# A selective scan whose delta·u·B product is formed on two engines

## The chip, the core and the metric

The program runs on one core of a Trainium2 chip. Time is the device time of one execution in microseconds (us). Before the change the median of three runs is 3355.29 us (3349.27 to 3361.40).

A core has a matrix engine (TensorE, PE in the profile; PEld is its weight load), VectorE (DVE), ScalarE (ACT), GpSimd (POOL) and SyncE (SP), each with an instruction stream of its own, which wait for one another on semaphores. TensorE writes to PSUM. VectorE and ScalarE read and write PSUM and SBUF; the GpSimd instructions of this kernel read and write SBUF alone.

## The reference, cut to what matters

The whole program is sixteen residual layers. The change is inside the first, a selective state-space scan (Mamba):

```
deltaA  = exp(delta * a)                # b l d n
deltaBu = delta * B * u                 # b l d n
step:  h = deltaA_t * h + deltaBu_t     # over the 256 positions of a sequence
       y = sum_n h * C_t
```

There are 8 sequences of 256 positions (2048 tokens), 256 inner channels d and 16 states n. B and C depend on token and state and are the same for every channel; delta and u depend on token and channel.

## The kernel before, in words

Channels lie on the 128 partitions, in M = 2 halves. Tokens are taken in 4 chunks c of C = 512 columns (two sequences each). For each chunk and each of the 16 states n there is one step q = 16 c + n, so there are Q = 64 steps. A step works on tiles of 128 partitions by 2 x 512 = 1024 columns:

- **TensorE** `spread` copies one row of B (then of C) to all 128 partitions with three bf16 matmuls of 512 columns, into the PSUM tiles `BB` and `CB` (L2431). There is one `BB` and one `CB`, so the next `spread` into `BB` waits until the product of the step before has read it. TensorE also sums the products with C over the 16 states into the PSUM tile `Y` (L2466, two float32 matmuls, four records), two steps late.
- **ScalarE** forms `dA[q]` = exp(delta · a) in two instructions (L2478), released when scan q-2 is done, and then copies `CB` to SBUF, `cb[q]` (L2484).
- **VectorE** forms `dBu[q]` = du · B with one `tensor_tensor` over all 1024 columns, which reads `du` from SBUF and `BB` from PSUM (`times_b`, L2518), and runs the recurrence with one `tensor_tensor_scan` (`scan`, L2527). It issues `times_b(q+1)` ahead of `scan(q)`.
- **GpSimd** forms `hc[q]` = hs · cb over 1024 columns in SBUF (L2493), after scan q.

`dBu`, `hs`, `cb`, `dA` and `hc` are double buffered. After the second step of each later chunk VectorE finishes the chunk before (`finish`: L2538, then L2543, whose two inputs `yv` and `gate` are both in SBUF). At steps 22, 38 and 54 TensorE projects that chunk into `BB` (`outputs`, L2440 and L2442) and VectorE adds it to x (`add_x`, L2548); there VectorE issues `scan(q)`, `add_x`, `times_b(q+1)` in that order. The last chunk is finished behind the loop. Nothing but the order in which each engine's block is written, and the semaphores, sets the order of the work.

## Time and profile before

| | |
|---|---|
| median of 3 runs | 3355.29 us |
| profiled execution, its own time | 3366.05 us |
| its span | 3364.3 us |
| mean granted TensorE clock | 0.894 |
| busy PE / DVE / ACT / POOL | 2804.9 / 2007.6 / 1387.5 / 962.4 us |

The span is from the first to the last instruction of the profiled execution. The scan stage that the change touches takes about 117 to 377 us of it; the other fifteen layers and the first half of this one take the rest and are not touched. In the rows below a line number is one of the kernel before; `x64` is a count; a time in square brackets behind a row of the timeline is how long the engine had been idle and who released it.

### The profile page before, as it was taken

The numbers are of one execution on the slowest core, as the hardware profiler recorded it, in microseconds if no ns is written. First come the engines' busy times: TensorE is split into PE (matmuls) and PEld (weight loads), VectorE is DVE, ScalarE is ACT, GpSimd is POOL, SyncE is SP. The second block draws the span as 40 slices with busy tenths as digits, with TensorE's granted clock in tenths as the row PEclk, the third lists the DMA queues.
The fourth block names the chain that finished last, engine by engine and source line by source line (L and its number), as shares of the span: only waits on it lengthen the run. The fifth ranks groups of instructions, "written<-read, shape, count | busy, mean of one in ns | idle before, by whom it ended". The sixth has DMA issues, their size and how long they took to land. (4 is left out here: it accounts for less than half of the span.)

```text
span 3364.3 us, 61234 instructions
## 1 busy us (share of the span) xinstructions
PE 2804.9 (83%) x23920; PEld 1857.1 (55%) x23920; DVE 2007.6 (60%) x4357; ACT 1387.5 (41%) x2886; POOL 962.4 (29%) x1321
## 2 busy tenths in 40 slices
PE   5589699979699969887687699996999969689996
PEld 2233367756477645555454566763566646456664
DVE  4999754556655566733465356665666646556664
ACT  4444244434244333322253244443555524345553
POOL 1355332223323220103213333331122235412222
PEclk7799799989799978777798799997999979799998
DMA  1000100000000000002010000001122101022221
GB/s 77 1 0 0 51 1 1 1 23 27 1 1 1 1 1 1 1 1 83 17 27 17 19 1 1 1 1 52 55 70 80 60 22 33 15 69 77 69 77 43
DMA packets 46939, 90.95 MB, mean 27 GB/s; under 512 B 6052, under 2 KB 34524, under 8 KB 45888
## 3 DMA queue, kind: packets, MB, share of 16 engines
q1 hardware_dynamic: 44608, 86.43, 8.4%
q8 instruction: 194, 3.18, 0.4%
q0 software_dynamic: 2048, 0.61, 0.1%
q14 instruction: 89, 0.73, 0.1%
HBM read 70.16 MB, written 19.14 MB: 27 GB/s over the span
## 5 line engine op out<-in xcount | busy, mean ns | idle before, releaser
L751 ACT ACTIVATE s_sT<-s_R 128x1024 f32<-128x1024 f32 (+2 forms) x448 | 400.1, 945 | 197.9 <-PE s_R L685 197.0
L786 DVE TENSOR_REDUCE s_negm<-s_R 128x4 f32<-128x1024 f32 x320 | 377.1, 1221 | 174.6 <-PE s_R L656 174.6
L656 PE MATMUL s_R<-s_qk 32*128 32x256 f32 (+2 forms) x3584 | 250.1, 394 | 62.7 <-ACT s_sT L751 33.5
L685 PE MATMUL s_R<-s_qA,s_qk 32*128 32x256 f32 (+2 forms) x3584 | 241.5, 383 | 16.1 <-DVE s_negm L786 10.7
L704 PE MATMUL s_OB<-s_sT,s_v 128*32 128x256 f32 (+2 forms) x3584 | 224.6, 368 | 10.0 <-ACT s_sT L751 6.4
L758 ACT ACTIVATE s_oc<-s_OB 128x256 f32<-128x256 f32 x224 | 86.0, 384 | 333.7 <-PE s_OB L704 333.7
L656 PEld LDWEIGHTS s_R<-s_qk 32*128 32x128 f32 x3584 | 158.7, 191 | 110.8 <-issue 88.5
L801 DVE TENSOR_TENSOR s_qA<-s_qk,s_X 128x256 f32<-128x256 f32 x224 | 94.3, 421 | 200.2 <-PE s_X L716 200.2
L2493 POOL TENSOR_TENSOR all_hT<-s0s_hs,s0s_cb 128x1024 f32<-128x1024 f32 x64 | 150.6, 2354 | 199.4 <-DVE s0s_hs L2527 182.2
L685 PEld LDWEIGHTS s_R<-s_qA,s_qk 32*128 32x128 f32 x3584 | 162.9, 185 | 78.4 <-issue 64.1
L1375 POOL TENSOR_TENSOR s_pr<-s_pr,s_rinv 128x1024 f32<-128x1024 f32 x64 | 121.3, 1895 | 224.7 <-DVE s_rinv L1481 224.7
L1453 ACT ACTIVATE s_pr<-s_S,s_negmax 128x256 f32<-128x256 f32 x256 | 118.7, 471 | 135.2 <-DVE s_negmax L1484 135.2
L791 DVE TENSOR_REDUCE s_negm<-s_R 128x2 f32<-128x256 f32 (+2 forms) x256 | 116.3, 518 | 68.2 <-PE s_R L666 68.1
L704 PEld LDWEIGHTS s_OB<-s_sT,s_v 128*32 128x32 f32 x3584 | 94.3, 109 | 106.7 <-issue 28.6
L2527 DVE TENSOR_TENSOR_SCAN s0s_hs<-s0s_dA,s0s_dBu 128x1024 f32<-128x1024 f32 x64 | 145.7, 2281 | 0.0
L2466 PE MATMUL s0s_Y<-all_hT,all_ident 128*128 128x512 f32 x256 | 129.7, 631 | 9.0 <-DVE s0s_yv L2538 6.3
L767 POOL TENSOR_SCALAR_AFFINE_SELECT s_sT<-s_sT 128x512 f32<-128x512 f32 x128 | 81.5, 637 | 176.7 <-ACT s_sT L751 174.7
L716 PE MATMUL s_X<-all_ident,s_negm 128*128 128x128 f32 x448 | 97.7, 300 | 14.5 <-DVE s_negm L786 7.6
L1064 POOL TENSOR_TENSOR s_veps<-s_mv,all_eps 128x2 f32<-128x2 f32 x64 | 16.7, 261 | 323.1 <-DVE s_mv L1266 323.1
L2431 PE MATMUL s0s_BB<-s0s_xparts,all_ident_bf 80*128 80x512 bf16 x192 | 57.9, 414 | 57.6 <-DVE s0s_xparts L2510 41.5
L1484 DVE TENSOR_REDUCE s_negmax<-s_S 128x4 f32<-128x1024 f32 x64 | 78.3, 1223 | 37.4 <-PE s_S L1393 37.4
L2484 ACT ACTIVATE s0s_cb<-s0s_CB 128x512 f32<-128x512 f32 x64 | 38.3, 598 | 138.3 <-PE s0s_CB L2431 137.1
(571 smaller groups left out, 6284.6 us busy)
## 6 DMA issues: line engine op xcount, KB each, us to landing
s_wB<-enc_b SPq DMA_DIRECT2D x32, 962.5 KB, 4.9
s_scratch<-s_pk SPq DMA_DIRECT2D x51, 256.0 KB, 2.0
s_qk<-s_scratch SPq DMA_DIRECT2D x204, 64.0 KB
s_wA<-enc_a SPq DMA_DIRECT2D x32, 193.0 KB, 4.1
big<-moe SPq DMA_DIRECT2D x2, 2347.0 KB, 11.2
big<-routed SPq DMA_DIRECT2D x2, 2084.0 KB
all_W<-weights SPq DMA_DIRECT2D x1, 2296.0 KB, 17.1
all_W<-weights SPq DMA_DIRECT2D x1, 2295.5 KB, 12.1
```

The source lines that it names most:

```text
L656: last = pe.matmul(S[h][:, t * T:t * T + hi - lo], b.qk[rows, r % 2, 0, c, t * P:(t + 1) * P], b.qk[rows, r % 2, 1, c, lo:hi], start=(t == ...
L685: last = pe.matmul(b.R[:, a.turned_at(u, h // 2), :][:, h % 2, a.at(kt)], b.qk[rows, r % 2, 1, c, kt * P:(kt + 1) * P], b.qA[rows, u % 2, ...
L704: last = pe.matmul(b.OB[32 * h:32 * (h + 1), lo:hi], b.v[:, r % 2, kt, a.HP * c + h, :], b.sT[:, j % (a.lag + 1), h, a.at(kt)], start=(kt ...
L716: last = pe.transpose(b.X[:, t * P:(t + 1) * P], b.negm[:, u % 2, t, :], g.ident[:])
L751: act.activation(b.sT[:, u % (a.lag + 1), 2 * p:2 * p + 2, 0:a.width], b.R[:, a.turned_at(u, p), 0:a.width], ACT.Exp).then_inc(s.expd, 1)
L786: ins = dve.tensor_reduce(b.negm[:, u % 2, :, at].rearrange("p t h -> p h t"), S.rearrange("p h (t k) -> p h t k", t=TT), AX_X, ALU.max, n ...
L791: ins = dve.tensor_reduce(b.negm[:, u % 2, t, at], S[:, :, t * T:t * T + hi - lo], AX_X, ALU.max, negate=True)
L1375: pool.tensor_tensor(p, p, rinv[:, u % 3, :, :].rearrange("p h t -> p (h t)").unsqueeze(2) .to_broadcast([P, 2 * TT, T]), ALU.mult).then_i ...
L1453: ins = act.activation(pr[:, u % 3, h, t, :], S[:, u % 2, h, t * T:(t + 1) * T], ACT.Exp, bias=negmax[:, u % 3, h, t:t + 1], accum_out=sum ...
L2466: last = pe.matmul(Y[:, m, :], g.ident[:], hc[:, j % 2, m, :], start=first, stop=last_)
L2493: pool.tensor_tensor(hc[:, q % 2, :, :], hs[:, q % 2, :, :], cb[:, q % 2, :].unsqueeze(1).to_broadcast([P, M, C]), ALU.mult)\
L2527: dve.tensor_tensor_scan(out=hs[:, q % 2, :, :].rearrange("p m c -> p (m c)"), data0=dA[:, q % 2, :, :].rearrange("p m c -> p (m c)"), dat ...
```

## The change

`bb` is a new SBUF tile of 128 x 2 x 144. ScalarE copies columns 368 to 511 of `BB` into it (`copy_b`), once per step, between its `exp` instructions and its copy of `CB`. GpSimd multiplies these 144 columns of both halves (288 of the 1024) by the copy (`times_b_high`), issued ahead of its `hc` product of the step before; VectorE's `times_b` keeps columns 0 to 367 (736 of 1024). The semaphore `dbu` becomes `dbu_low` and `dbu_high`, and `scan` waits for both. `times_b` now waits for ScalarE's copy (`bb_cp`), no longer for the matmuls, and TensorE waits for `dbu_low` alone before it overwrites `BB`.

```diff
--- before.py
+++ after.py
@@ -2401,6 +2401,8 @@
             dBu = ss.sb("dBu", [P, 2, M, C])
             hs = ss.sb("hs", [P, 2, M, C])
             cb = ss.sb("cb", [P, 2, C])
+            CUT = 368
+            bb = ss.sb("bb", [P, 2, C - CUT])
             xparts = ss.sb("xparts", [ROWS, 3, NTOK], BF16)
 
             hc = g.hT[:, 0:2 * M * C].rearrange("p (i m c) -> p i m c", i=2, m=M)
@@ -2410,9 +2412,9 @@
             BB = ss.ps("BB", [P, C])
             CB = ss.ps("CB", [P, C])
             Y = ss.ps("Y", [P, M, C])
-            split, cleared, bb_mm, cb_mm, cb_cp, exps, dbu, scans, hcs, summed, gated, out_mm, added = [
-                ss.sem(n) for n in ("split", "cleared", "bb_mm", "cb_mm", "cb_cp", "exps", "dbu", "scans", "hcs",
-                                    "summed", "gated", "out_mm", "added")]
+            (split, cleared, bb_mm, bb_cp, cb_mm, cb_cp, exps, dbu_low, dbu_high, scans, hcs, summed, gated, out_mm,
+             added) = [ss.sem(n) for n in ("split", "cleared", "bb_mm", "bb_cp", "cb_mm", "cb_cp", "exps", "dbu_low",
+                                           "dbu_high", "scans", "hcs", "summed", "gated", "out_mm", "added")]
             Q = NC_ * N
 
             def segments(t):
@@ -2447,7 +2449,7 @@
                     spread(BB[:], 0, 32, bb_mm)
                     for q in range(Q + 2):
                         if q + 1 < Q:
-                            pe.wait_ge(dbu, q + 1)
+                            pe.wait_ge(dbu_low, q + 1)
                             if (c := projects(q)) is not None:
                                 outputs(c)
                                 pe.wait_ge(added, c + 1)
@@ -2469,6 +2471,13 @@
 
                 @block.scalar
                 def _(act):
+                    def copy_b(q):
+                        act.wait_ge(bb_mm, q + 1)
+                        if q >= 2:
+                            act.wait_ge(dbu_high, q - 1)
+                        act.activation(bb[:, q % 2, :], BB[:, CUT:C], ACT.Copy).then_inc(bb_cp, 1)
+
+                    copy_b(0)
                     act.wait_ge(cleared, 1)
                     for q in range(Q):
                         c, n = divmod(q, N)
@@ -2478,6 +2487,8 @@
                             ins = act.activation(segments(dA[:, q % 2, m, :]), segments(delta[:, m, c * C:(c + 1) * C]),
                                                  ACT.Exp, scale=aneg[:, m * N + n:m * N + n + 1])
                         ins.then_inc(exps, 1)
+                        if q + 1 < Q:
+                            copy_b(q + 1)
                         act.wait_ge(cb_mm, q + 1)
                         if q >= 2:
                             act.wait_ge(hcs, q - 1)
@@ -2485,7 +2496,20 @@
 
                 @block.gpsimd
                 def _(pool):
+                    def times_b_high(q):
+
+                        c = q // N
+                        pool.wait_ge(bb_cp, q + 1)
+                        if q >= 2:
+                            pool.wait_ge(scans, q - 1)
+                        pool.tensor_tensor(dBu[:, q % 2, :, CUT:C], du[:, :, c * C + CUT:(c + 1) * C],
+                                           bb[:, q % 2, :].unsqueeze(1).to_broadcast([P, M, C - CUT]), ALU.mult)\
+                            .then_inc(dbu_high, 1)
+
+                    times_b_high(0)
                     for q in range(Q):
+                        if q + 1 < Q:
+                            times_b_high(q + 1)
                         pool.wait_ge(cb_cp, q + 1)
                         pool.wait_ge(scans, q + 1)
                         if q >= 2:
@@ -2512,16 +2536,18 @@
                     def times_b(q):
 
                         c = q // N
-                        dve.wait_ge(bb_mm, q + 1)
+                        dve.wait_ge(bb_cp, q + 1)
                         if q >= 2:
                             dve.wait_ge(scans, q - 1)
-                        dve.tensor_tensor(dBu[:, q % 2, :, :], du[:, :, c * C:(c + 1) * C],
-                                          BB[:].unsqueeze(1).to_broadcast([P, M, C]), ALU.mult).then_inc(dbu, 1)
+                        dve.tensor_tensor(dBu[:, q % 2, :, 0:CUT], du[:, :, c * C:c * C + CUT],
+                                          BB[:, 0:CUT].unsqueeze(1).to_broadcast([P, M, CUT]), ALU.mult)\
+                           .then_inc(dbu_low, 1)
 
                     def scan(q):
 
                         dve.wait_ge(exps, q + 1)
-                        dve.wait_ge(dbu, q + 1)
+                        dve.wait_ge(dbu_low, q + 1)
+                        dve.wait_ge(dbu_high, q + 1)
                         if q >= 2:
                             dve.wait_ge(hcs, q - 1)
                         dve.tensor_tensor_scan(out=hs[:, q % 2, :, :].rearrange("p m c -> p (m c)"),
```

## Rows read from the trace of the kernel before

**Rows 1.** Groups by line and shape, 100 to 380 us: busy, mean ns | idle before, releasers.

```profile
L2493 POOL TENSOR_TENSOR all_hT<-s0s_hs,s0s_cb 128x1024 f32<-128x1024 f32 x64 | 150.6, 2354 | 199.4 <-DVE s0s_hs L2527 182.2 <-PE s0s_Y L2466 16.0 <-ACT s0s_cb L2484 1.2
L2527 DVE TENSOR_TENSOR_SCAN s0s_hs<-s0s_dA,s0s_dBu 128x1024 f32<-128x1024 f32 x64 | 145.7, 2281 | 0.0
...
L2518 DVE TENSOR_TENSOR s0s_dBu<-s_du,s0s_BB 128x1024 f32<-128x1024 f32 x64 | 78.1, 1221 | 22.7 <-PE s0s_BB L2431 16.9 <-DVE s0s_hs L2527 0.5
...
L2484 ACT ACTIVATE s0s_cb<-s0s_CB 128x512 f32<-128x512 f32 x64 | 38.3, 598 | 138.3 <-PE s0s_CB L2431 137.1 <-POOL all_hT L2493 1.2
```

**Rows 2.** Timeline of one steady step, all engines: start us, us, engine, instruction.

```profile
226.13 1.30 ACT L2478 ACTIVATE s0s_dA<-s_delta,s_aneg 128x510 f32<-128x510 f32 x2
226.20 1.22 DVE L2518 TENSOR_TENSOR s0s_dBu<-s_du,s0s_BB 128x1024 f32<-128x1024 f32 x1
226.23 2.35 POOL L2493 TENSOR_TENSOR all_hT<-s0s_hs,s0s_cb 128x1024 f32<-128x1024 f32 x1 [1.17 <-DVE s0s_hs L2527]
227.33 2.28 DVE L2527 TENSOR_TENSOR_SCAN s0s_hs<-s0s_dA,s0s_dBu 128x1024 f32<-128x1024 f32 x1
...
227.47 0.82 PE L2431 MATMUL s0s_BB<-s0s_xparts,all_ident_bf 80*128 80x512 bf16 x3 [0.34 <-DVE s0s_dBu L2518]
...
228.13 0.81 PE L2431 MATMUL s0s_CB<-s0s_xparts,all_ident_bf 80*128 80x512 bf16 x3
...
228.78 1.88 PE L2466 MATMUL s0s_Y<-all_hT,all_ident 128*128 128x512 f32 x4
228.98 0.60 ACT L2484 ACTIVATE s0s_cb<-s0s_CB 128x512 f32<-128x512 f32 x1 [1.55 <-PE s0s_CB L2431]
...
229.72 1.22 DVE L2518 TENSOR_TENSOR s0s_dBu<-s_du,s0s_BB 128x1024 f32<-128x1024 f32 x1
```

**Rows 3.** Timeline of PE alone where it catches up.

```profile
274.19 0.81 PE L2431 MATMUL s0s_BB<-s0s_xparts,all_ident_bf 80*128 80x512 bf16 x3
...
277.21 0.81 PE L2431 MATMUL s0s_BB<-s0s_xparts,all_ident_bf 80*128 80x512 bf16 x3
```

**Rows 4.** Groups by shape, POOL, whole span.

```profile
L1088 POOL TENSOR_TENSOR s_x1b<-s_x,s_wB 128x256 f32<-128x256 f32 x32 | 21.3, 667 | 2.5
...
L2942 POOL TENSOR_TENSOR s1a_oh<-s1a_oh,s_sig 128x128 f32<-128x128 f32 x32 | 14.0, 438 | 0.0
...
L1370 POOL TENSOR_TENSOR all_x<-all_x,all_W 128x2048 f32<-128x2048 f32 x1 | 4.5, 4508 | 3.0 <-SPq L1367 3.0
```

**Rows 5.** Groups by shape, DVE and ACT, whole span.

```profile
L358 DVE TENSOR_TENSOR s_sT<-s_S,all_causal 128x512 f32<-128x512 f32 x32 | 21.7, 680 | 0.0
...
L2905 ACT ACTIVATE s1a_v<-s1a_F 128x256 f32<-128x256 f32 x32 | 12.3, 384 | 87.4 <-PE s1a_F L2807 87.4
```

**Rows 6.** Timeline at the finish of the first and of the last chunk.

```profile
184.58 2.35 POOL L2493 TENSOR_TENSOR all_hT<-s0s_hs,s0s_cb 128x1024 f32<-128x1024 f32 x1 [1.55 <-DVE s0s_hs L2527]
185.77 2.24 DVE L2543 TENSOR_TENSOR s0s_yv<-s0s_yv,s_gate 128x1024 f32<-128x1024 f32 x1
...
376.07 1.23 DVE L2543 TENSOR_TENSOR s0s_yv<-s0s_yv,s_gate 128x1024 f32<-128x1024 f32 x1
```

**Rows 7.** Timeline of DVE where it waited for `BB`.

```profile
131.30 1.22 DVE L2518 TENSOR_TENSOR s0s_dBu<-s_du,s0s_BB 128x1024 f32<-128x1024 f32 x1 [0.55 <-PE s0s_BB L2431]
...
212.09 1.22 DVE L2518 TENSOR_TENSOR s0s_dBu<-s_du,s0s_BB 128x1024 f32<-128x1024 f32 x1 [4.59 <-PE s0s_BB L2431]
...
275.05 1.22 DVE L2518 TENSOR_TENSOR s0s_dBu<-s_du,s0s_BB 128x1024 f32<-128x1024 f32 x1 [1.79 <-PE s0s_BB L2431]
```

**Rows 8.** Timeline of the last steps, DVE and POOL.

```profile
365.49 4.46 DVE L2527 TENSOR_TENSOR_SCAN s0s_hs<-s0s_dA,s0s_dBu 128x1024 f32<-128x1024 f32 x2
...
367.91 4.64 POOL L2493 TENSOR_TENSOR all_hT<-s0s_hs,s0s_cb 128x1024 f32<-128x1024 f32 x2 [1.18 <-DVE s0s_hs L2527]
```

**Rows 9.** Busy us by stretch: PE, PEld, DVE, ACT, POOL, granted clock, DMA share, GB/s.

```profile
117.00:370.00 253.00, 227.93 (x703) 93.54 (x701) 231.21 (x140) 117.32 (x190) 148.03 (x63) 0.92 0.00 0
...
184.00:192.00 8.00, 6.12 (x11) 2.42 (x12) 7.86 (x7) 1.85 (x4) 2.88 (x2) 0.57 0.00 0
```

## The prediction

> **What bounds the kernel now.** I read first the groups by line of the scan stage [rows 1], because the change touches nothing else: the 64 steps are in 117 to 370 us, 253 us of a span of 3364.3. In that stretch VectorE is busy 231.2 us and TensorE 227.9, at a mean granted clock of 0.92; GpSimd 148.0 and ScalarE 117.3 [rows 9]. Two engines near the full time don't say which one sets the pace, so I read the timeline of one step [rows 2]. VectorE's product starts at 226.20 and the next one at 229.72: 3.52 us per step. Between them it does 1.22 us of product and 2.28 us of scan, one right behind the other (the scan's record begins 0.09 before the product's ends; the next product begins 0.11 after the scan's end, 229.61). VectorE never waits: the scan group has 0.0 us of idle time before it over 64 instructions, and the product group 22.7 us, most of it at a few places [rows 1]. All others wait in each step: GpSimd 1.17 us for the scan, ScalarE 1.55 us for `CB`, TensorE 0.34 us for the product. So a steady step is VectorE's own work, and a shorter product shortens the step one for one until another engine becomes late. That next engine is to be found. TensorE, when it catches up without a wait at the full clock, needs 277.21 - 274.19 = 3.02 us per step [rows 3]. GpSimd needs 2.354 us, ScalarE 1.30 + 0.60 = 1.90.
>
> **What the change takes from VectorE.** Its product goes from 1024 to 736 columns. Two sizes with one PSUM and one SBUF operand are at hand: 1221 ns for 1024 [rows 1], 680 for 512 [rows 5]; that is 1.057 ns per column, and 1221 - 288 x 1.057 = 917 ns. I take 0.92 us, a gain of 0.30 us per step; the step of VectorE becomes 3.22 us. Bounds: if all of the time shrank with the columns the gain would be 0.34, and it can't be much under 288 x 1.0 ns = 0.29.
>
> **What it adds to GpSimd.** A product over 288 columns in SBUF. Sizes: 128 columns 438 ns, 256 columns 667, 2048 columns 4508 [rows 4]; from the last two, 2.14 ns per column and 118 ns fixed, so 118 + 617 = 735 ns. Lower bound 288 x 2.2 = 0.63 us (the longest piece's cost per column, nothing fixed), upper bound 288 x 3.42 = 0.99 us (the smallest piece's cost per column). I take 0.74, as 288 lies beside 256. Two GpSimd products run back to back without a gap, 4.64 us for two [rows 8], so GpSimd's step is 2.354 + 0.74 = 3.09 us, below VectorE's 3.22 with 0.13 to spare. At the upper bound it is 3.34, and GpSimd would be the bound.
>
> The Trainium skill's "GPSIMD Engine Reference", section "Engine selection", says to keep elementwise work on VectorE because two-input operations are about twice as slow on GpSimd. The rows above agree in the ratio (0.74 us for what VectorE does in 0.30, as one price against the other); by that rule the change loses 0.44 us of engine time per step, and by the row on GpSimd's 1.17 us of idle time that loss is covered.
>
> **What it adds to ScalarE.** A copy of 144 columns from PSUM: 256 columns take 384 ns [rows 5] and 512 take 598 [rows 1], 0.836 ns per column, so 290 ns. ScalarE's step is 1.90 + 0.29 = 2.19 us, far below 3.22. The question is the order. Count from E, the end of scan q-1, behind which `times_b(q+1)` should begin at E + 0.11. `times_b(q)` ended at about E - 2.2; the matmuls of `BB` follow at once and take 0.82 us [rows 2], so they end at E - 1.3, and the copy runs to E - 1.0. It stands behind exp(q) in ScalarE's queue; that was released by scan q-2 at E - 3.2 and is over at E - 1.9. The copy is thus 1.0 us early. Queued behind it is the copy of `CB` (its matmuls end at E - 0.7, so it starts when it did) and then the next exp, released at E. TensorE is free for `BB` in time: it waits for `hc`, which now ends 2.35 + 0.14 after a scan as before, and its 3.02 us fit in 3.22.
>
> **GpSimd's order.** Its stream is now `times_b_high(q+1)`, `hc(q)`. `hc(q-1)` starts at E + 0.14 and ends at E + 2.49, the new piece ends at E + 3.23, and `hc(q)` is released by scan q at E + 3.22 + 0.14. So it is just in time, 0.13 us early. Scan q+1, which needs the piece, starts some 0.9 us after its end: covered. If the piece costs p, the step is the larger of 3.22 and 2.354 + p.
>
> **A lock.** VectorE's L2543 has two SBUF inputs. It takes 1.23 us when GpSimd is idle and 2.24 us when it starts at 185.77 during a GpSimd product that ends at 186.93; 186.93 + 1.08 is its end [rows 6]. So it is held until the GpSimd product is over. VectorE's product in each step starts 0.03 us before a GpSimd product and still takes 1.22 [rows 2]: with one operand in PSUM it isn't held. The Trainium skill's "SBUF — State Buffer", section "SBUF: two separate sides", has the same rule: VectorE with two SBUF inputs and GpSimd exclude each other for a whole instruction, others don't. By rule and row the new piece holds up nothing in the steady step; what it can hold up is L2543, if GpSimd takes its new piece ahead of the waiting VectorE: between 0 and 0.74 us at three places. I take half, 0.37.
>
> **The sum.** Of the 64 products these gain nothing: the first five, up to 131.30, where `BB` comes late from a TensorE at the lower clock [rows 7] and where each product now also waits 0.04 + 0.29 us for the copy; and at each of the three projections two: the first is followed by a wait for the next `BB` anyway, the second waits for `BB` (4.59 us, 1.79 us [rows 7], and 3.33 at the third) and pays 0.33 for the copy while it gains 0.30. That leaves 64 - 5 - 6 = 53 x 0.30 = 15.9 us. Against it: at the three projections scan 22 follows scan 21 without a product between; it would begin 0.11 + 0.84 + 2.18 = 3.13 us after scan 20 ends, and its GpSimd piece is done at 3.28: 0.15, say 0.2 with the rest, three times 0.6. At the three finishes 0.37 for the lock, and 0.2 because TensorE is at half clock there (0.57 in that stretch [rows 9]) and the copy comes behind late `BB` matmuls: 1.7. At the end the chain is scan 62, then two `hc` back to back [rows 8]: unchanged. Net 15.9 - 0.6 - 1.7 = 13.6 us. The profiled execution took 3366.05 us (span 3364.3) and would take 3352.5; it was 10.8 above the median of the runs, and off the median of 3355.29 the forecast is 3341.7, rounded to 3342.
>
> **Rivals.**
> A, GpSimd becomes the bound. At p = 0.99 the step is 3.34, a gain of 0.18 x 53 = 9.5 less 2.3 = 7.2 us: 3348. For it: the spare is 0.13 us only, and the piece has runs of 144 columns and a repeated operand. Against it: the row for 256 columns. Chance 0.2.
> B, something else takes the gain back and the time is the same, 3355: the wait of scan on two engines and of `times_b` on ScalarE adds 0.3 us per step, for example if a wait that is already satisfied costs time at VectorE. Against it: now three waits stand ahead of each scan and it starts before the product's record ends [rows 2]. Chance 0.09.
> C, the other side: the granted clock. At the lower of the two levels (1.2 GHz) TensorE's step is twice 3.02, so 6.04 us against 3.22, 2.8 us lost per step; the two projections with 4.59 and 1.79 us of wait show the same 2.8 [rows 7]. The clock fell where TensorE had paused at a finish. To come out 10 us slower, eight more steps than now (13.6 + 10 = 23.6, over 2.8) would have to run at half clock: 3365. Against it: TensorE will be idle 0.2 us of 3.22 and not 0.5 of 3.52, so it pauses less. A smaller dose, one or two steps either way, is 3 to 6 us of the range. Chance 0.06.
> D, more than forecast: the denser TensorE keeps its clock at the projections, which saves up to 2.8 + 1.5 us, and L2543 isn't held longer: 3336. Chance 0.1.
> The forecast itself: 0.55.
>
> **How the numbers follow.** A difference of 0.3%, 10 us, is about what a measurement of this kernel tells from no change. Faster by more, under 3345.2: most of the forecast (0.49 of 0.55; its own spread is about 4 us), all of D, a fifth of A: 0.63. Slower by more: C and a little for what I don't see, 0.07. Same: 0.30. The range goes from 3332 (gain 0.34 per step, D) to 3356 (A and B inside).
>
> **What would show it.** In the profile after: VectorE's product about 0.92 us; product to product 3.22 in a steady step, with no idle time before the scan; GpSimd's piece about 0.74 and its idle time before `hc` near 0.1 us, released by the scan; ScalarE's copy 0.29, over 1 us before the next product. Wrong if idle time stands before the scan with GpSimd as its releaser (A), if the gaps inside a step grow with no releaser (B), or if stretches of the stage are at half clock that weren't (C).

## The result, and the profile after

| | median, us | runs | profiled execution | span | granted clock |
|---|---|---|---|---|---|
| before | 3356.66 (3349.27 to 3361.4) | 4 | 3366.05 | 3364.3 | 0.894 |
| changed | 3333.1 (3332.89 to 3338.31) | 4 | 3333.2 | 3331.5 | 0.899 |

The ratio is 0.9937, with a 95% interval from 0.9919 to 0.9955: 23.6 us less between the medians, where 13.6 was forecast and 3342 predicted. The two profiled executions differ by more, 32.8 us, because that of before lies 9.4 above its median.

The share of busy time by engine in the changed kernel (the page's first part):

```profile
PE 2787.0 (84%) x23920; PEld 1851.9 (56%) x23920; DVE 1989.3 (60%) x4357; ACT 1404.2 (42%) x2950; POOL 1010.8 (30%) x1385
```

The groups by line and shape of the changed kernel in the same stretch as [rows 1], 100 to 380 us. Its product is now L2542, its scan L2553, `hc` L2517, the copy of `CB` L2495; new are the piece on GpSimd, L2505, and the copy of `B`, L2478:

```profile
L2517 POOL TENSOR_TENSOR all_hT<-s0s_hs,s0s_cb 128x1024 f32<-128x1024 f32 x64 | 150.6, 2353 | 28.1 <-DVE s0s_hs L2553 14.6 <-PE s0s_Y L2468 7.7
L2553 DVE TENSOR_TENSOR_SCAN s0s_hs<-s0s_dA,s0s_dBu 128x1024 f32<-128x1024 f32 x64 | 146.1, 2283 | 1.2 <-POOL s0s_dBu L2505 1.2
L2542 DVE TENSOR_TENSOR s0s_dBu<-s_du,s0s_BB 128x736 f32<-128x736 f32 x64 | 58.9, 921 | 24.2 <-ACT s0s_bb L2478 18.4 <-DVE s0s_hs L2553 0.5
L2505 POOL TENSOR_TENSOR s0s_dBu<-s_du,s0s_bb 128x288 f32<-128x288 f32 x64 | 53.8, 841 | 100.9 <-ACT s0s_bb L2478 100.9
...
L2478 ACT ACTIVATE s0s_bb<-s0s_BB 128x144 f32<-128x144 f32 x64 | 18.6, 290 | 94.9 <-PE s0s_BB L2433 94.9
```

The product fell from 1221 to 921 ns. The scan kept its 2.28 us and waits 1.2 us in all 64 steps together. GpSimd's wait for the scan ahead of `hc` went from 182.2 us [rows 1] to 14.6: its idle time was filled. (The mean of 841 ns for the piece holds three of 1.78 us, at the finishes; nearly all of the 100.9 us ahead of L2505 is idle time from before the stage.)

One steady step of the changed kernel, all engines, against [rows 2]:

```profile
226.09 0.92 DVE L2542 TENSOR_TENSOR s0s_dBu<-s_du,s0s_BB 128x736 f32<-128x736 f32 x1
226.12 2.35 POOL L2517 TENSOR_TENSOR all_hT<-s0s_hs,s0s_cb 128x1024 f32<-128x1024 f32 x1
226.93 2.28 DVE L2553 TENSOR_TENSOR_SCAN s0s_hs<-s0s_dA,s0s_dBu 128x1024 f32<-128x1024 f32 x1
...
227.98 0.29 ACT L2478 ACTIVATE s0s_bb<-s0s_BB 128x144 f32<-128x144 f32 x1 [0.66 <-PE s0s_BB L2433]
...
228.43 0.80 POOL L2505 TENSOR_TENSOR s0s_dBu<-s_du,s0s_bb 128x288 f32<-128x288 f32 x1
...
229.32 0.92 DVE L2542 TENSOR_TENSOR s0s_dBu<-s_du,s0s_BB 128x736 f32<-128x736 f32 x1
229.35 2.35 POOL L2517 TENSOR_TENSOR all_hT<-s0s_hs,s0s_cb 128x1024 f32<-128x1024 f32 x1
```

Product to product it is 3.23 us, with no idle time on VectorE. The copy of `B` ends at 228.27, 1.05 us before the product that follows. GpSimd's piece ends at 229.23 and the next `hc` starts at 229.35: 0.12 us of spare.

The scan stage in the sense used from here on runs from the start of the first product to the end of the last gating product (L2543 before, L2569 after). It took 259.81 us before (117.49 to 377.30) and 242.97 after (114.44 to 357.41): 16.8 less. What follows it, the other fifteen layers above all, took 2987.0 us before and 2974.1 after, though not one of their instructions was changed; another 3.1 us lie ahead of the stage, in code that is the same too. So there are two questions: why 16.8 and not 13.6, and where the rest came from.

### The profile page after: what moved, and what is told of

It is laid out like the page before. It is cut to its first block and busy times, and to the rows that moved or that the text cites. A ratio compares the mean times of both kernels' runs of the same rounds, so it can differ in the third digit from the quotient of the medians.

```text
span 3331.5 us, 61548 instructions
## 1 busy us (share of the span) xinstructions
PE 2787.0 (84%) x23920; PEld 1851.9 (56%) x23920; DVE 1989.3 (60%) x4357; ACT 1404.2 (42%) x2950; POOL 1010.8 (30%) x1385
## 3 DMA queue, kind: packets, MB, share of 16 engines
q0 software_dynamic: 2048, 0.61, 0.1%
## 5 line engine op out<-in xcount | busy, mean ns | idle before, releaser
L786 DVE TENSOR_REDUCE s_negm<-s_R 128x4 f32<-128x1024 f32 x320 | 377.3, 1221 | 172.2 <-PE s_R L656 172.2
L801 DVE TENSOR_TENSOR s_qA<-s_qk,s_X 128x256 f32<-128x256 f32 x224 | 94.3, 421 | 200.8 <-PE s_X L716 200.8
L2517 POOL TENSOR_TENSOR all_hT<-s0s_hs,s0s_cb 128x1024 f32<-128x1024 f32 x64 | 150.6, 2353 | 28.1 <-DVE s0s_hs L2553 14.6
L704 PEld LDWEIGHTS s_OB<-s_sT,s_v 128*32 128x32 f32 x3584 | 94.2, 109 | 106.7 <-issue 28.6
L2553 DVE TENSOR_TENSOR_SCAN s0s_hs<-s0s_dA,s0s_dBu 128x1024 f32<-128x1024 f32 x64 | 146.1, 2283 | 1.2 <-POOL s0s_dBu L2505 1.2
L1064 POOL TENSOR_TENSOR s_veps<-s_mv,all_eps 128x2 f32<-128x2 f32 x64 | 16.6, 260 | 323.0 <-DVE s_mv L1266 323.0
L716 PEld LDWEIGHTS s_X<-all_ident,s_negm 128*128 128x128 f32 x448 | 45.5, 142 | 81.1 <-issue 30.1
```

What stands on the lines that cost most here:

```text
L704: last = pe.matmul(b.OB[32 * h:32 * (h + 1), lo:hi], b.v[:, r % 2, kt, a.HP * c + h, :], b.sT[:, j % (a.lag + 1), h, a.at(kt)], start=(kt ...
L716: last = pe.transpose(b.X[:, t * P:(t + 1) * P], b.negm[:, u % 2, t, :], g.ident[:])
L786: ins = dve.tensor_reduce(b.negm[:, u % 2, :, at].rearrange("p t h -> p h t"), S.rearrange("p h (t k) -> p h t k", t=TT), AX_X, ALU.max, n ...
L801: dve.tensor_tensor(b.qA[:, u % 2, :], b.qk[:, r % 2, 0, c, :], b.X[:, 0:T], ALU.add).then_inc(s.x_used, 1)
L2517: pool.tensor_tensor(hc[:, q % 2, :, :], hs[:, q % 2, :, :], cb[:, q % 2, :].unsqueeze(1).to_broadcast([P, M, C]), ALU.mult)\
L2553: dve.tensor_tensor_scan(out=hs[:, q % 2, :, :].rearrange("p m c -> p (m c)"), data0=dA[:, q % 2, :, :].rearrange("p m c -> p (m c)"), dat ...
```

## The experiments

All of them but the last two are compared with the kernel before on the same chip, whose median over a session of 15 to 25 runs was 3355.78, 3354.19 and 3361.32 us. The last two are compared with each other. In the table "scan stage" and "behind it" are those two stretches of the profiled execution.

| kernel | median (runs), us | ratio to before | scan stage | behind it |
|---|---|---|---|---|
| before, first profile | | | 259.81 | 2987.0 |
| before, again | 3357.37 (12) | 1.0006 [0.9992, 1.0021] | 259.69 | 2979.9 |
| changed, again | 3327.22 (6) | 0.9923 [0.9903, 0.9942] | 242.97 | 2968.4 |
| copy and wait alone | 3356.94 (10) | 1.0006 [0.9993, 1.0019] | 261.96 | 2983.3 |
| cut at 440 | 3337.58 (6) | 0.9950 [0.9930, 0.9969] | 248.35 | 2970.9 |
| cut at 304 | 3332.27 (4) | 0.9934 [0.9919, 0.9949] | 254.83 | 2967.7 |
| cut at 352 | 3322.11 (5) | 0.9908 [0.9894, 0.9921] | 243.00 | 2969.9 |
| changed + 18.5 us pause | 3346.81 (11) | 0.9982 [0.9973, 0.9991] | 241.62 | 2985.0 (2966.5 without the pause) |
| changed + 9.2 us pause | 3340.94 (5) | 0.9961 [0.9948, 0.9975] | 241.46 | 2983.6 (2974.4 without) |
| before + 9.2 us pause | 3360.04 (12) | 1.0002 [0.9991, 1.0013] | 259.78 | 2976.8 (2967.6 without) |
| piece not used | 3353.78 (12) | 0.9980 [0.9968, 0.9992] | 260.32 | 2974.9 |
| before, first layer alone | 391.25 (5) | | | |
| changed, first layer alone | 374.61 (5) | | | |

**The two kernels once more**, without an edit, for the spread of stages between executions.

> The kernel before once more, timed against itself. It says how far two series of one kernel lie apart, and gives a second profile. Theory S (the whole gain of 23.6 us lies in the scan stage, which became 17 us shorter, and the rest of the profiles' difference is what the granted clock happened to do): ratio 1.000 within 0.002, the median somewhere in 3349 to 3361, and in the new profile the layers behind the first take other times than in the first profile by several us, linear attention (147.6 us there) above all. Theory D (the layers behind the first got faster by 5 us or more because they start earlier): the layers behind the first repeat the first profile within 2 us, linear attention again 147.6.

> The changed kernel once more. Both theories: 3333 to 3338, ratio 0.9937 within its interval (0.9919 to 0.9955). Scan stage: steady step 3.225 us, product 0.921, GpSimd piece 0.80. Theory S: the whole first layer 358 to 361 us (377.1 before, 358.6 in the first profile), and the ratio of five rounds nearer 0.9945 (18.5 us) than 0.993. Theory D: the ratio stays at 0.993 and the layers behind the first repeat the first profile, linear attention 140.4.

The scan stage repeats to 0.12 us and 0.00 us, so its 16.8 isn't chance between executions. (With other code behind it, in the two kernels with a pause and in the first layer alone, the stage of the changed kernel takes 241.5 to 241.6 us, 1.4 less; the part on the mis-sized terms says why.) What lies behind it came out 11.5 us apart (2979.9 and 2968.4). Neither theory held as written: linear attention repeated to 0.1 us, but all that lies behind the stage differs between two executions of one kernel by 7.1 us before and 5.7 after. (The expectations give linear attention as 147.6 and 140.4 us, up to the next layer's normalization; the table further down counts that too, 159.0 and 151.7.) The scan stage starts at 117.49 and 116.35 in the kernel before and at 114.44 and 112.72 in the changed one, though all that lies ahead of it is the same: 3.1 and 3.6 us of difference; the pair with the first layer alone (below) tells what to think of that.

**The copy and the wait alone.** ScalarE copies and VectorE's product waits for the copy, but VectorE does all 1024 columns and GpSimd nothing new; the semaphore `dbu_high` and the waits for it are left out.

```diff
-                        pool.tensor_tensor(dBu[:, q % 2, :, CUT:C], du[:, :, c * C + CUT:(c + 1) * C],
-                                           bb[:, q % 2, :].unsqueeze(1).to_broadcast([P, M, C - CUT]), ALU.mult)\
-                            .then_inc(dbu_high, 1)
...
-                        dve.tensor_tensor(dBu[:, q % 2, :, 0:CUT], du[:, :, c * C:c * C + CUT],
-                                          BB[:, 0:CUT].unsqueeze(1).to_broadcast([P, M, CUT]), ALU.mult)\
+                        dve.tensor_tensor(dBu[:, q % 2, :, :], du[:, :, c * C:(c + 1) * C],
+                                          BB[:].unsqueeze(1).to_broadcast([P, M, C]), ALU.mult)\
```

> The handshake alone: ScalarE copies the 144 columns of B as in the changed kernel and VectorE waits for the copy, but VectorE forms all 1024 columns itself and GpSimd has no piece. The copy is read by nobody; output as before. If the wait costs nothing in a steady step because the copy is 1.0 us early, the step is 3.52 us as before, product 1.22, and the total is the one of the kernel before plus 0.33 us at about eight places (start, projections): plus 2 to 3 us, ratio 1.000 to 1.001. If the wait costs something in each step (rival), the step is over 3.55 and the total over plus 5 us.

Scan and product of this kernel, 100 to 380 us:

```profile
L2545 DVE TENSOR_TENSOR_SCAN s0s_hs<-s0s_dA,s0s_dBu 128x1024 f32<-128x1024 f32 x64 | 145.7, 2281 | 0.0
L2535 DVE TENSOR_TENSOR s0s_dBu<-s_du,s0s_BB 128x1024 f32<-128x1024 f32 x64 | 78.1, 1221 | 25.2 <-ACT s0s_bb L2476 19.4 <-DVE s0s_hs L2545 0.5
```

The idle time before the product is 2.5 us more than in [rows 1], at the places where `BB` is late anyway, and the stage is 2.2 us longer. The steady step is 3.53 us (145.24 to 148.77). The product's wait, already satisfied, costs nothing that can be read here. The scan's second wait isn't in this kernel; it is in "piece not used" below, with the same step of 3.52 us. Together they rule out rival B.

**Other cuts.** `CUT = 368` becomes 440, 304 and 352; nothing else.

> GpSimd takes 72 of 512 columns (144 of 1024) in place of 144. VectorE bound: product 1221 - 144 x 1.04 = 1.07 us, step 3.375 us, half of the gain. Theory S: gain in the first layer 53 to 58 x 0.15 = 8 to 9 us, total near 3347. Theory D or a clock effect that grows with it: total gain 12 us. GpSimd's piece about 0.45 to 0.49 us, its idle time before the product with C 0.4 us per step.

> GpSimd takes 208 of 512 columns (416 of 1024). Its piece costs 0.80 + 128 x 0.00214 = 1.07 us, so its step is 2.31 + 1.07 = 3.38 us and, with no spare left, about 3.4 with the hand-over; VectorE needs only 3.09. If the step is the larger of the two sums, it is now GpSimd bound at 3.38 to 3.5, idle time before the product with B or the scan has GpSimd or ScalarE as releaser, and the scan stage loses some 0.2 x 53 = 10 us of the changed kernel's gain (243.0 us there, some 252 here). Rival (GpSimd is never late, VectorE's own work sets the step whatever the split): 3.09 and a stage 7 us shorter than the changed kernel's.

> GpSimd takes 160 of 512 columns (320 of 1024): VectorE 704 columns 0.888 us, step 3.19; GpSimd 0.80 + 0.07 = 0.87, step 2.31 + 0.87 = 3.18. Balanced. If the step is the larger of the two sums: 3.19 to 3.2, 0.033 x 53 = 1.7 us less than the changed kernel in the stage, a total not to be told from it. If GpSimd needs the spare of 0.1 us for the hand-over: 3.22 to 3.26, the same or 2 us more. A change of the total beyond 3 us either way would be the clock in later layers.

At 440 the product takes 1.07 us and the step 3.38; the stage is 11.5 us shorter than before, where 56 steps of 0.15 give 8.4, and the total is 18.2 less, more than either theory had. At 352 the step is 3.19 and the stage the same 243.0. The 0.03 us a step are lost at the projections: the product waits 14.8 us there in all, 13.4 in the changed kernel, and the scan 1.6 in the whole stage, for 1.2. At 304 GpSimd is the bound; its steady step:

```profile
145.38 2.35 POOL L2517 TENSOR_TENSOR all_hT<-s0s_hs,s0s_cb 128x1024 f32<-128x1024 f32 x1
...
147.68 1.08 POOL L2505 TENSOR_TENSOR s0s_dBu<-s_du,s0s_bb 128x416 f32<-128x416 f32 x1
...
148.01 0.79 DVE L2542 TENSOR_TENSOR s0s_dBu<-s_du,s0s_BB 128x608 f32<-128x608 f32 x1
...
148.71 2.35 POOL L2517 TENSOR_TENSOR all_hT<-s0s_hs,s0s_cb 128x1024 f32<-128x1024 f32 x1
148.96 2.29 DVE L2553 TENSOR_TENSOR_SCAN s0s_hs<-s0s_dA,s0s_dBu 128x1024 f32<-128x1024 f32 x1 [0.16 <-DVE s0s_dBu L2542]
```

`hc` to `hc` is 3.33 us with nothing idle on GpSimd. The scan, which used to start before the product's end, starts 0.16 us behind it. The profile names the product as its releaser, but the piece ended at 148.76, 0.04 before that, and the scan starts 0.20 behind the piece. That is the delay with which it follows a late piece elsewhere too (0.20 us behind the piece's end at three places of the changed kernel): it is GpSimd that releases it. So the step is the larger of two sums. GpSimd's is 2.30 from the start of `hc` to the piece and 1.03 from there to the next `hc`, 3.33 in all; the records overlap by 0.04. A piece of 320 columns takes 0.87, so the two sums come near each other at the cut at 352, where the step of 3.19 is still VectorE's own work. At 304 rival A is true.

The longer step is only half of what this kernel's stage loses. It is 11.9 us longer than the changed kernel's, and 5.0 of these lie at the three finishes, where the gating product takes 3.91 us in place of 2.23 (the lines are shown under "The lock"). The whole kernel, at 0.9934 of before, is as fast by its median as the changed one in the first comparison (0.9937), though its stage gains only 5.0 us of 260. The profiles don't account for that in full: behind the stage it has 6.4 us less than the first profile of the changed kernel and 0.7 less than the second, and the execution that was profiled lay 7.0 us above its median. So of the 21.9 us between this kernel's median and that of before, some 17 don't come from the stage.

**The first layer alone.** In both kernels one line is changed; the outputs leave out the other fifteen layers.

```diff
-layers=range(16)
+layers=range(1)
```

> The kernel before, cut to its first layer (load, layer norm, the layer with the scan, store; the other fifteen layers are left out). Something near 430 us. It is the reference for the next run: with no later layers, the difference of the two is the scan stage (259.8 us against 243.0 in the profiles) and the 95 us ahead of it, whose code is the same.

> The changed kernel, cut to its first layer in the same way. If the scan stage alone carries the gain and the rest of the 23 to 29 us comes from the later layers: 16.8 us less than the run before, 15.5 to 18. If the 2 us that the changed kernels were faster ahead of the scan (they reached the first product at 112.7 to 116.8 us, the others at 116.4 to 117.5) belong to the change: 18 to 20 less. The forecast's own sum for this stage was 13.6.

First product and last gating product of the kernel before, cut to its first layer:

```profile
114.78 1.22 DVE L2518 TENSOR_TENSOR s0s_dBu<-s_du,s0s_BB 128x1024 f32<-128x1024 f32 x1 [1.55 <-PE s0s_BB L2431]
...
373.23 1.22 DVE L2543 TENSOR_TENSOR s0s_yv<-s0s_yv,s_gate 128x1024 f32<-128x1024 f32 x1
```

and of the changed kernel, cut likewise:

```profile
114.88 0.92 DVE L2542 TENSOR_TENSOR s0s_dBu<-s_du,s0s_BB 128x736 f32<-128x736 f32 x1 [1.88 <-ACT s0s_bb L2478]
...
355.18 1.22 DVE L2569 TENSOR_TENSOR s0s_yv<-s0s_yv,s_gate 128x1024 f32<-128x1024 f32 x1
```

The scan stage is 259.67 and 241.52 us, 18.2 less, and starts at nearly the same time in both, 0.1 us apart: that it began some 3 us earlier in the whole changed kernel isn't put down to the change (with the short pause behind it, the same code starts the stage at 116.84). Of the 18.2, 1.3 is lost again outside the stage, nearly all of it behind: the spans differ by 16.8 (389.5 and 372.7) and the medians by 16.6 (ranges 390.81 to 393.15 and 372.81 to 375.89). That is the change's own gain. The rest of the 23.6 (and of the 28.6 of the second comparison), 7 to 12 us, arises in code that the change doesn't touch. By the two pairs of profiles 3.1 and 3.6 us lie ahead of the stage, and 12.9 and 11.5 behind it; they add up to more than the medians' rest because the first profile of before was a long one.

**Where the rest lies.** The length of some later layers, from a layer's first VectorE instruction to the next layer's, in us:

| layer | before, twice | copy and wait alone | before + pause | piece not used | changed, twice | changed + 18.5 us |
|---|---|---|---|---|---|---|
| linear attention | 159.0, 159.0 | 161.9 | 151.6 | 151.7 | 151.7, 151.7 | 151.7 |
| second routed attention | 313.2, 313.1 | 310.6 | 311.0 | 311.1 | 310.9, 310.9 | 310.9 |
| first mixture of experts | 97.5, 94.3 | 94.2 | 93.5 | 96.5 | 96.8, 91.2 | 92.6 |
| second mixture of experts | 108.8, 105.9 | 105.6 | 108.0 | 108.4 | 108.6, 105.6 | 106.8 |

Linear attention holds 7.3 of it. Its granted clock, in stretches of 8 us from 16 us after its first instruction, in the kernel before (columns as in [rows 9]):

```profile
1273.70:1281.70 8.00, 8.00 (x81) 5.16 (x78) 6.11 (x11) 2.83 (x6) 0.00 (x0) 0.81 0.00 0
1281.70:1289.70 8.00, 6.82 (x44) 3.98 (x42) 4.47 (x8) 1.85 (x4) 0.00 (x0) 0.62 0.01 2
1289.70:1297.70 8.00, 8.00 (x61) 4.46 (x64) 4.06 (x9) 2.94 (x6) 0.00 (x0) 0.53 0.00 0
1297.70:1305.70 8.00, 6.83 (x72) 4.58 (x72) 5.86 (x11) 3.22 (x7) 0.00 (x0) 0.90 0.01 2
```

and the same stretches of the layer in the changed kernel:

```profile
1251.50:1259.50 8.00, 8.00 (x53) 4.57 (x52) 4.66 (x6) 2.22 (x5) 0.00 (x0) 0.50 0.00 0
1259.50:1267.50 8.00, 6.82 (x84) 4.59 (x80) 5.60 (x12) 2.84 (x7) 0.00 (x0) 1.00 0.01 2
1267.50:1275.50 8.00, 8.00 (x112) 5.31 (x100) 7.29 (x16) 4.20 (x10) 0.00 (x0) 1.00 0.01 2
```

The same instructions stand in the same order in both. In the kernel before, the clock rises earlier (0.81 in the first row, where the changed kernel still has 0.50), falls back to its lower level, 1.2 GHz, for most of the next two stretches, and rises again. In the changed kernel it rises later and stays at 2.4 GHz. In the second profile of the kernel before, the clock changes at the same times after the layer's start, to 0.1 us, and so it does in the second one of the changed kernel: this isn't chance between executions.

**Pauses.** If the rest comes from when the later layers run or from what ran ahead of them, a pause behind the scan stage can take it away or give it. VectorE repeats one product of 128x2048 (2.29 us each, 2.33 from start to start), whose result nobody uses, 8 or 4 times behind the last `add_x`; all later layers wait for it. From that `add_x` to the next layer's first instruction it is 20.6 us with 8 and 11.3 with 4, for 2.15 without: the pauses are 18.5 and 9.2 us long, a little less than the expectations took. The edit is shown for 8; with 4 it was made in both kernels.

```diff
                     finish(NC_ - 1)
                     add_x(NC_ - 1)
+                    dve.wait_ge(scans, Q)
+                    for i in range(8):
+                        if i:
+                            dve.wait_ge(pad, i)
+                        dve.tensor_tensor(dBu[:].rearrange("p i m c -> p (i m c)"), du[:, 0, :], delta[:, 0, :],
+                                          ALU.mult).then_inc(pad, 1)
```

> The changed kernel with a pause of eight extra VectorE products (results unused), 8 x 2.35 = 19 us, behind the scan stage's last instruction; all later layers then begin where they begin in the kernel before. Theory D (the later layers run on another pattern of the granted clock because they begin 19 us earlier): they take what they take in the kernel before, linear attention 159 us and not 152, layers behind the first 2957 to 2964 in all and not 2945 to 2951, total 3333 + 19 + 8 or so, near 3355. Theory S (the later layers differ by chance from one profile to the next): linear attention 152 or 159 at random, total 3327 to 3333 + 19 = 3346 to 3352. Rival R (what counts is the state in which the first layer leaves the clock, not when): linear attention stays at 152, total 3346 to 3352.

> The same with four extra products, 9.4 us. Theory D: later layers begin about 3 us later than in the kernel with 440 columns on VectorE, which had 152.7 us for linear attention; something between 151 and 162 us, the total not on a straight line between the changed kernel and the one with the long pause. Theories S and R: total 3327 to 3333 + 9.4, 3337 to 3342, linear attention 152 (R) or at random (S).

> The kernel before with the pause of four extra VectorE products (9.4 us) behind its scan stage. So far the layers behind the first took 2957 to 2965 us in the profiles of the three kernels without a GpSimd piece, and 2943 to 2951 us in the seven profiles with one, whatever the pause. Theory T (what counts is the time at which the later layers begin): here they begin 9.4 us later than ever, and their sum leaves 2957 to 2965, linear attention isn't 159 us. Theory P (what counts is that GpSimd's stream has 64 more instructions, or another property of the program that a pause doesn't change): 2957 to 2965, linear attention 159, total 3356 + 9.4 = 3365.

The kernel before with 9.2 us added takes the same time as without: 3360.04 against 3361.32, as theory T has it. Its later layers gave the 9.2 back. Linear attention takes 151.6 us there, and the clock in its stretches of 8 us, again from 16 us on:

```profile
1279.30:1287.30 8.00, 8.00 (x80) 4.94 (x77) 5.82 (x11) 2.83 (x6) 0.00 (x0) 0.76 0.00 0
1287.30:1295.30 8.00, 6.83 (x82) 4.51 (x81) 5.98 (x13) 3.22 (x7) 0.00 (x0) 1.00 0.01 2
1295.30:1303.30 8.00, 7.20 (x82) 4.62 (x80) 7.65 (x15) 3.87 (x9) 0.00 (x0) 1.00 0.01 2
```

It rises as early as in the kernel before (0.76) and stays up as in the changed one. The changed kernel with 18.5 us added begins its second layer when the kernel before does (385.7 us, for 386.5 and 385.3), reaches linear attention at 1253.9, within 4 us of when the kernel before does (1257.7 and 1256.3), and takes 151.7 us for it all the same, against theory D:

```profile
1269.90:1277.90 8.00, 8.00 (x52) 4.57 (x52) 4.66 (x6) 2.21 (x5) 0.00 (x0) 0.50 0.00 0
1277.90:1285.90 8.00, 6.83 (x84) 4.59 (x80) 5.59 (x12) 2.83 (x7) 0.00 (x0) 0.99 0.01 2
```

With more than the stage's gain given back it is still faster than before, 0.9982 [0.9973, 0.9991]. In the changed kernel the pauses cost 13.7 to 19.6 us for 18.5 and 7.8 to 13.7 for 9.2, by which of its two medians (3333.1 and 3327.22) is subtracted. What is unusual, then, is the kernel before: it has the slow pattern, and the pause takes it out. Not every small edit does: the kernel with the copy alone takes 161.9 us.

**The piece not used.** GpSimd forms its piece as in the change, but into a tile that nobody reads, and VectorE forms all 1024 columns: GpSimd's new work without the shorter step.

```diff
+            unused = ss.sb("unused", [P, 2, M, C - CUT])
...
-                        pool.tensor_tensor(dBu[:, q % 2, :, CUT:C], du[:, :, c * C + CUT:(c + 1) * C],
+                        pool.tensor_tensor(unused[:, q % 2, :, :], du[:, :, c * C + CUT:(c + 1) * C],
```

> The changed kernel's ScalarE copy and GpSimd piece stay, but the piece is written to a spare tile that nobody reads, and VectorE forms all 1024 columns. So the program is nearly the changed one, at the old step of 3.52 us. Scan stage 260 to 262 us as in the kernel with the wait alone. Theory P: the later layers take 2943 to 2951 us, linear attention 152, and the total is some 10 us under the kernel before, near 3346, though the step didn't get shorter. Theory Q (the gain behind the first layer hangs on the shorter step): 2957 to 2965, linear attention 159 to 162, total 3357 as with the wait alone.

The step is 3.52 us as before (145.15 to 148.68), though GpSimd works beside it:

```profile
147.49 0.80 POOL L2506 TENSOR_TENSOR s0s_unused<-s_du,s0s_bb 128x288 f32<-128x288 f32 x1
...
148.68 1.22 DVE L2543 TENSOR_TENSOR s0s_dBu<-s_du,s0s_BB 128x1024 f32<-128x1024 f32 x1
148.71 2.35 POOL L2518 TENSOR_TENSOR all_hT<-s0s_hs,s0s_cb 128x1024 f32<-128x1024 f32 x1 [0.42 <-DVE s0s_hs L2554]
```

The stage is 260.3 us, so GpSimd's piece doesn't lengthen VectorE's step. The whole kernel is 0.9980 [0.9968, 0.9992] of before, 7.5 us, with nothing gained in the stage; linear attention takes 151.7. The 16.6 us of the change alone and these 7.5 add up to 24.1, where the first comparison has 23.6 and the second 28.6, so that the sum comes out may be chance. This run is what theory P forecast, but GpSimd's longer stream can't be needed for the fast pattern: the kernel before with a pause has no piece and has it too.

**What stays open**: which event ahead of a layer chooses the pattern of its clock. The long values, 159.0 and 161.9, are those of the kernel before and of the copy alone; all other kernels have 151.6 to 154.8, among them one with the step of the kernel before and no piece (before + pause), one with that step and the piece (piece not used), and ones that reach the layer at about the same time. Neither the step nor GpSimd's stream sorts them. The start of the layer isn't excluded: it is at 1256.3, 1257.4 and 1257.7 us in the three profiles with long values and nowhere between 1255.1 and 1263.2 in the nine others (the nearest are 1255.0, piece not used, and 1263.3, before + pause). Against it speaks that the two profiles of the kernel before start the layer 1.3 us apart and agree to 0.1 us. No run moved the start alone in steps this small, and of most kernels only one profile is at hand.

## Why the prediction was right, and where its sum was short

**The bound.** Right: the steady step went from 3.52 to 3.23 us, VectorE's own work, with no idle time inside. Product 921 ns (0.92), saving 0.30 us (0.30).

**GpSimd's piece.** 0.80 us where 0.74 was taken from 256 and 2048 columns; within its bounds. It starts 2.31 us after `hc` starts, not 2.354, so the spare came out at 0.12 against the 0.13 forecast: two small errors cancel. The cut at 304 shows rival A's mechanism with a longer piece.

**ScalarE's copy.** 0.290 us (0.29), over 1.05 us before the product needs it (1.0). Right, and alone it costs nothing in the steady step.

**The lock.** Wrong in who is held, for this kernel. The second finish of the changed kernel:

```profile
235.80 2.35 POOL L2517 TENSOR_TENSOR all_hT<-s0s_hs,s0s_cb 128x1024 f32<-128x1024 f32 x1
237.00 2.23 DVE L2569 TENSOR_TENSOR s0s_yv<-s0s_yv,s_gate 128x1024 f32<-128x1024 f32 x1
...
238.10 1.78 POOL L2505 TENSOR_TENSOR s0s_dBu<-s_du,s0s_bb 128x288 f32<-128x288 f32 x1
...
239.15 0.91 DVE L2542 TENSOR_TENSOR s0s_dBu<-s_du,s0s_BB 128x736 f32<-128x736 f32 x1
```

VectorE's gating product waits for `hc` as in [rows 6] and takes the same 2.23. When `hc` ends, it goes ahead, and GpSimd's piece is the one held: 1.78 us and not 0.80, at all three finishes. Nobody waits for the piece there, because the product of VectorE follows only at 239.15. So 3 x 0.37 = 1.1 us of the sum were not paid.

With the cut at 304 it is the other way round, at all three finishes of that kernel:

```profile
178.73 2.35 POOL L2517 TENSOR_TENSOR all_hT<-s0s_hs,s0s_cb 128x1024 f32<-128x1024 f32 x1
179.28 3.91 DVE L2569 TENSOR_TENSOR s0s_yv<-s0s_yv,s_gate 128x1024 f32<-128x1024 f32 x1
...
181.04 1.06 POOL L2505 TENSOR_TENSOR s0s_dBu<-s_du,s0s_bb 128x416 f32<-128x416 f32 x1
183.11 0.77 DVE L2542 TENSOR_TENSOR s0s_dBu<-s_du,s0s_BB 128x608 f32<-128x608 f32 x1
```

The gating product starts 1.8 us before the piece can, is passed by it, and ends at 183.19, 1.09 behind the piece's end; it takes 3.91, 3.91 and 3.92 us, 1.68 more each time. The prediction's mechanism, GpSimd taking its piece ahead of the waiting VectorE, is thus real, and at this cut it costs the whole piece and more. The Trainium skill's "SBUF — State Buffer", section "Who interferes with whom", says that the order of issue decides who is blocked; the trace of the changed kernel agrees (VectorE issued at 237.00, 1.1 us before GpSimd's piece could), that of the cut at 304 does not. What decides is open. The gating product starts 1.2 us after `hc` where it goes ahead (cuts at 440, 368 and 352, three times each) and 0.5 after it where it is passed; no run set this apart from the length of the piece. That the changed kernel pays nothing here was luck, as far as the prediction goes. The same section of the Trainium skill also names VectorE's two-port modes among what contends with GpSimd, which "others don't" in the prediction leaves out; no row here shows one.

**The three projections.** The scan behind them is held 0.21, 0.57 and 0.21 us, for 0.2 each in the sum, and once more, 0.21, at the last step. Three times it follows the piece's end by 0.20; the second time by 0.56, and nothing in the trace says what held it for the other 0.36. The first and the longest of these in the changed kernel, with the waits of the product for `BB` beside them:

```profile
193.17 2.29 DVE L2553 TENSOR_TENSOR_SCAN s0s_hs<-s0s_dA,s0s_dBu 128x1024 f32<-128x1024 f32 x1 [0.21 <-POOL s0s_dBu L2505]
...
200.29 0.92 DVE L2542 TENSOR_TENSOR s0s_dBu<-s_du,s0s_BB 128x736 f32<-128x736 f32 x1 [2.09 <-ACT s0s_bb L2478]
...
252.51 2.29 DVE L2553 TENSOR_TENSOR_SCAN s0s_hs<-s0s_dA,s0s_dBu 128x1024 f32<-128x1024 f32 x1 [0.57 <-POOL s0s_dBu L2505]
```

**The terms that were mis-sized.** VectorE's accounts of the stage, before [rows 1] against after, close the gap. All 64 products are shorter by 0.30: 19.2 us. The sum let only 53 of them count, which is to say that idle time before the product would take back 11 x 0.30 = 3.3. It took back 24.2 - 22.7 = 1.5: 1.8 us better. The finishes cost nothing where 1.7 was forecast: 1.7 better. Waits before the scan are 1.2 where 0.6 stood: 0.6 worse. That leaves 0.3 for durations in which the two profiles differ. 13.6 + 1.8 + 1.7 - 0.6 + 0.3 = 16.8.

Of the 1.8, 1.6 is the clock at the projections. There the product waits 13.4 us in all, 13.2 before, where the sum let idle time grow by 1.8. At the full clock the two waits of a projection are 2.71 us before and 3.33 after, 0.62 more; with one stretch of 3.4 us at 1.2 GHz they are 4.40 and 5.02, the same 0.62 more. But the kernel before had such a stretch at one projection and twice its length at another (6.09 us of waits), and the changed kernel had one at two projections and the longer one nowhere. In the kernels with a pause and in the first layer alone only one projection of the changed stage has it: 11.7 us of waits in place of 13.4, hence the stage of 241.5. The 0.6 that stood for half clock at the finishes, a part of the 1.7, is the clock too, as far as the runs tell: no product waits behind a finish in any profile of the changed kernel, which is at 1.2 GHz there for 3.4 us at most, while with the copy and 6.8 us of the lower clock behind a finish the product waits 0.9 us once (copy and wait alone, piece not used, and the cut at 440). The stage of the changed kernel, and the stretch around its first finish that begins as long before the gating product as the row of [rows 9] for 184 to 192 us:

```profile
114.00:358.00 244.00, 224.00 (x714) 92.90 (x713) 214.78 (x143) 136.72 (x256) 202.05 (x128) 0.96 0.00 1
176.24:184.24 8.00, 5.05 (x14) 1.94 (x14) 7.86 (x8) 3.55 (x7) 5.37 (x4) 1.00 0.00 0
```

The mean clock is 0.96 for 0.92 before, and around the first finish 1.00 for 0.57. Behind its start (from 130 us on) the stage is at 1.2 GHz for 7 us in all five profiles of the changed kernel, for 20 to 31 in the four of the kernel before, for 17 to 18 with the copy alone and with the piece not used, and for 14, 17 and 24 with the cuts at 440, 352 and 304. What rival D said of the clock and of the lock was thus true in part beside the forecast's own mechanism, and rival C (the clock falls more often) went the other way. The cause that D gives, a denser TensorE, isn't shown: around the first finish TensorE is busy less of the 8 us than before (5.05 for 6.12, at the full clock for 0.57), and the cut at 304 has a shorter step than before and hardly less of the lower clock. No run took this apart.

**What no step of the prediction had.** All that the change doesn't touch was taken as unchanged. It gave 7 to 12 us, the larger part of the miss in the total (10.0 us of gain, 23.6 for 13.6); the change alone, with 16.6, missed by 3.0. The first comparison can't tell this from the change's gain: only the layer alone, the pauses and the unused piece could. So there is luck in how near the total came: 3333.1 us lies 1.1 above the lower end of the range, and the second series of the same kernel, 3327.22, lies below it.

**The shortest time.** The cut at 352 has the lowest median, 3322.11 us, 0.9908 [0.9894, 0.9921] of before, against 0.9923 [0.9903, 0.9942] for the change run again, in another session on another chip. It is faster than the kernel before; its interval overlaps the change's, its stage is equal to 0.03 us, and so it isn't shown to be faster than the changed kernel.

## What to carry to other kernels

Price work moved to an idle engine by the sum of each engine's step and take the larger one: here a piece that costs 0.80 us on GpSimd for 0.30 saved on VectorE pays because 1.17 us were idle, and the cut at 304 shows where it ends. The Trainium skill's "Perfetto Trace Analysis", section "Optimizing Scalar/DVE Operations", warns that moving work between these two engines might not help, since they share an SBUF read port; here it gave 16.6 us. The products of the steady step have one operand in PSUM and take their 0.92 us beside a running `hc`; where a gating product has two in SBUF, the piece was held 1 us with nobody waiting. At the cut at 304 the same spot cost 1.68 us three times, so look at each place where VectorE has two SBUF operands.

In a long kernel a difference of 0.2 or 0.3% in the total isn't yet the change's. Time the changed stage alone in a program cut down to it, and add a pause of the size of the gain behind it: if a pause costs nothing in one of the kernels, part of what you measured is a pattern of the clock in layers that nobody touched.

## What the runs showed of the hardware that was not expected

- A pause of 9.2 us on the path cost nothing in the kernel before (ratio 1.0002 [0.9991, 1.0013]).
- The same instructions of one layer take 151.7 or 159.0 us (161.9 once) depending on edits that end over 800 us earlier, and the two kernels that were profiled twice repeat their own value to 0.1 us. In the slower pattern of the kernel before the clock had risen sooner, and fell again twice.
- GpSimd's instructions follow each other without a gap: the piece starts 0.04 us before the record of `hc` ends.
- A VectorE product with two SBUF inputs that waits for the end of an `hc` went ahead of GpSimd's next piece three times of three in the changed kernel (the piece of 288 columns took 1.78 us instead of 0.80), and was passed by it three times of three with the cut at 304 (3.91 us instead of 2.23), though it had started first each time.
